# Normalising the last 17 layer norms on GpSimd in a four-layer gated kernel

## The reference, cut to what matters

```python
def _layernorm(x, axis=-1, eps=1e-05):
    m = jnp.mean(x, axis=axis, keepdims=True)
    v = jnp.var(x, axis=axis, keepdims=True)
    return (x - m) / jnp.sqrt(v + eps)

x = x + jnp.tanh(g_xattn[0]) * _L0_xattn_ref(_layernorm(x, axis=-1), ...)   # gated by token range
x = x + jnp.tanh(g_ffn[0]) * _L0_ffn_ref(_layernorm(x, axis=-1), ...)       # 64 experts, top 4, and shared
x = x + jnp.tanh(g_xattn[1]) * _L1_xattn_ref(_layernorm(x, axis=-1), ...)   # mLSTM heads
x = x + jnp.tanh(g_ffn[1]) * _L1_ffn_ref(_layernorm(x, axis=-1), ...)       # low rank, 8 experts
x = x + jnp.tanh(g_xattn[2]) * _L2_xattn_ref(_layernorm(x, axis=-1), ...)   # attention with a cache
x = x + jnp.tanh(g_ffn[2]) * _L2_ffn_ref(_layernorm(x, axis=-1), ...)       # ternary weights, 8-bit tokens
x = x + jnp.tanh(g_xattn[3]) * _L3_xattn_ref(_layernorm(x, axis=-1), ...)   # attention kept to the 54 best
x = x + jnp.tanh(g_ffn[3]) * _L3_ffn_ref(_layernorm(x, axis=-1), ...)       # ternary weights, relu squared
```

## Time and profile before

| what | value |
|---|---|
| median of 3 runs | 614.92 us (612.87 to 615.05) |
| profiled execution, its own time | 614.48 us |
| its span, first to last instruction | 612.7 us |
| TensorE (PE) busy | 459.0 us, 75% |
| VectorE (DVE) busy | 361.6 us, 59% |
| ScalarE (ACT) busy | 231.9 us, 38% |
| GpSimd (POOL) busy | 170.6 us, 28% |
| mean granted TensorE clock | 0.852 |

### The profile page before, as it was taken

The page is one execution under the profiler, slowest core; times in us unless marked ns, Lnnn a source line. Parts: engine busy times, 40 slices in busy tenths (PEclk is TensorE's granted clock), DMA queues, the critical chain, the costliest instruction groups (busy, mean ns, idle before and its releaser), DMA issues.

```text
span 612.7 us, 7209 instructions
## 1 busy us (share of the span) xinstructions
PE 459.0 (75%) x2538; PEld 332.1 (54%) x2546; DVE 361.6 (59%) x1021; ACT 231.9 (38%) x405; POOL 170.6 (28%) x165
## 2 busy tenths in 40 slices
PE   1999986949999026768987099999997676754664
PEld 0788862318887013435654067788873364633442
DVE  6463367961113363976555354422479999999844
ACT  1200036242243313345432032223467662334775
POOL 4000017783803675340425650000011010000200
PEclk9999969888999665769878569999999987966877
DMA  8860502113991510010001000000000000000001
GB/s 279 264 267 2 205 0 82 32 39 113 350 311 58 173 37 12 7 40 29 2 1 50 20 2 0 1 0 1 1 1 1 0 2 0 2 0 1 18 18 34
DMA packets 25124, 37.59 MB, mean 61 GB/s; under 512 B 5678, under 2 KB 20148, under 8 KB 25088
## 3 DMA queue, kind: packets, MB, share of 16 engines
q1 hardware_dynamic: 22016, 33.38, 16.0%
q0 software_dynamic: 3072, 3.75, 2.1%
HBM read 32.32 MB, written 9.44 MB: 68 GB/s over the span
## 4 chain that ended last, share of the span: by engine, by line
PE 45%; DVE 30%; POOL 10%; issue 7%; ACT 5%; DMA 2%; POOLq 0%; DVEq 0%; ACTq 0%
PE bank L1427 5%; PE bank L1514 5%; PE bank L1437 5%; PE bank L1747 3%; POOL ar L557 3%; POOL xg_rows L515 3%; PE bank L1536 3%; DVE top L1103 2%; DVE big L1100 2%; DVE HN L606 2%; PE bank L1761 2%; PE bank L1785 2%; PE bank L1769 2%; DVE bnst L596 2%; PE bank L1801 2%
## 5 line engine op out<-in xcount | busy, mean ns | idle before, releaser
L470 POOL TENSOR_TENSOR rstd<-ve,neghalf 128x2 f32<-128x2 f32 x32 | 24.9, 779 | 265.1 <-DVE ve L601 265.0
L515 POOL DMA_INDIRECT xg_rows<-HN,slot x32 | 33.1, 1033 | 21.8 <-DVE slot L727 12.6
L774 DVE TENSOR_TENSOR he<-sil,bank 64x64 f32<-64x64 f32 x32 | 7.0, 218 | 52.9 <-ACT sil L1192 52.7
L916 DVE TENSOR_TENSOR SH<-bank,HM 128x512 f32<-128x512 f32 x32 | 22.0, 689 | 24.4 <-ACT HM L1268 10.0
L557 POOL TENSOR_TENSOR ar<-ar,neghalf 128x32 f32<-128x32 f32 x4 | 21.7, 5431 | 41.1 <-DVE ar L880 41.1
L1468 PE MATMUL bank<-HT,SH 128*128 128x512 f32 x64 | 33.0, 674 | 0.0
L606 DVE TENSOR_SCALAR HN<-X,mv,rstd 128x256 f32<-128x256 f32 x64 | 26.9, 462 | 9.8 <-POOL rstd L470 9.6
L1514 PEld LDWEIGHTS bank<-ph,big 128*128 128x128 f32 x256 | 31.3, 193 | 1.3 <-issue 0.4
L1268 ACT ACTIVATE HM<-bank 128x512 f32<-128x512 f32 x32 | 19.1, 598 | 32.5 <-PE bank L1623 27.9
L1427 PE MATMUL bank<-HM,CT 128*128 128x256 f32 x128 | 30.2, 398 | 1.2 <-DVE HM L630 1.2
L1514 PE MATMUL bank<-ph,big 128*128 128x64 f32 x256 | 30.6, 273 | 0.0
(11 more groups left out here) (356 smaller groups left out, 1173.1 us busy)
## 6 DMA issues: line engine op xcount, KB each, us to landing
big<-in_ew SPq DMA_DIRECT2D x16, 768.0 KB, 6.4
xg_rows<-zer SPq DMA_DIRECT2D x1, 2048.0 KB, 8.4
ph<-xg_rows SPq DMA_DIRECT2D x16, 128.0 KB, 4.2
y_rows<-ph SPq DMA_DIRECT2D x16, 128.0 KB, 2.7
X<-in_x SPq DMA_DIRECT2D x4, 256.0 KB, 6.6
CT<-in_ctxT SPq DMA_DIRECT2D x1, 1024.0 KB, 7.6
CN<-in_ctx SPq DMA_DIRECT2D x1, 1024.0 KB, 11.6
ar<-in_q2g SPq DMA_DIRECT2D x1, 1024.0 KB, 4.8
```

The costliest lines, as they stand in the source:

```text
L470: pool.tensor_tensor(rstd[:, b, :], ve[:, b, :], neghalf[:, 0:TB], ALU.pow)\
L515: pool.indirect_dma_start(out=xg_dram, out_offset=bass.IndirectOffsetOnAxis(slot[:, t, k:k + 1], 0), in_=HN[:, t, :], in_offset=None, boun ...
L916: dve.tensor_tensor(cs[:, g, :], bank[i % 3][:], dcs[:, i % 2, :], ALU.mult).then_inc(s["s_cs"], 1)
```

## The change

The two tensor_scalar instructions of each of the 17 planned norms leave VectorE's program and stand in GpSimd's, directly behind the power whose result they use. GpSimd waits for its own power (`s_lnrstd`) before them and counts a new semaphore `s_gnorm`. TensorE's `turn` and VectorE's `quantise_tokens` wait for `s_gnorm` in place of `s_norm`. The steps `turn1`, `norm4` and `norm6` have no part of VectorE any more, so their nine turns leave VectorE's string in `TURNS_OF`; the order of all the other steps, on every engine, stays the same (the strings are only broken at other places). The load of `ctx` gives up its semaphore and counts as the fourth of the group `shared`, at its old place in the queue. The 15 norms ahead of the plan stay on VectorE.

```diff
--- before.py
+++ after.py
@@ -45,20 +45,20 @@
         (("in2a", "TVS"), ("in2b", "TVS"), ("round2", "VS"), ("turn2", "TS"), ("out2", "TV" if j < TB - 1 else "TVG"))]
 FFN3 = [((name, j), engines) for j in range(TB) for name, engines in
         (("in3", "TVS"), ("round3", "VS"), ("turn3", "TS"), ("out3", "TV"))]
-STEPS = ([("heads", "VG"), ("turn1", "TVS"), ("route1", "TVS"), ("low1", "TV"), ("lowturn1", "TS"), ("lowout1", "TVG"),
-          ("norm4", "TVS"), ("keys2", "TS"), ("values2", "TS"), ("scores2", "TVS"), ("probs2", "TS"), ("mix2", "TS"),
+STEPS = ([("heads", "VG"), ("turn1", "TS"), ("route1", "TVS"), ("low1", "TV"), ("lowturn1", "TS"), ("lowout1", "TVG"),
+          ("norm4", "TS"), ("keys2", "TS"), ("values2", "TS"), ("scores2", "TVS"), ("probs2", "TS"), ("mix2", "TS"),
           ("project2", "TVG"), ("norm5", "VSG"), ("turn5", "TS")] + FFN2 +
-         [("norm6", "TVS"), ("queries3", "TS"), ("scores3", "TVS"), ("clip3", "VS"), ("probs3", "TS"), ("mix3", "TS"),
+         [("norm6", "TS"), ("queries3", "TS"), ("scores3", "TVS"), ("clip3", "VS"), ("probs3", "TS"), ("mix3", "TS"),
           ("project3", "TVG"), ("norm7", "VSG"), ("turn7", "TS")] + FFN3)
 
 TURNS_OF = {
-    "T": ("021012130230130201230201320103123012313010232303112201023031031212013203231010302121313002"
-             "3023231110033311202012103130210213232323232"),
-    "V": ("012303123001132203312003101220301321021032013012312031023121302303213103032101201313021201"
-             "0130123232323232"),
-    "S": ("012130230012302012010312312301030231302101220132130321032013013212310203023101310102323231"
-             "310003230111201213013021032123232323232"),
-    "G": "3012300112233012300113322",
+    "T": ("02101213023013020123020132010312301231301023230311220102303103121201320323101030212131300230"
+          "23231110033311202012103130210213232323232"),
+    "V": ("01230123013203120031012203013210210320130123120312312302303110303210120131302120101301232323"
+          "23232"),
+    "S": ("01213023001230201201031231230103023130210122013213032103201301321231020302310131010232323131"
+          "0003230111201213013021032123232323232"),
+    "G": ("3012300112233012300113322"),
 }
 
 
@@ -336,7 +336,7 @@
                  "s_hcp s_hr16 s_v16 s_r16 s_hh s_wif0 "
                  "s_l1 s_nm1 s_ex1 s_ha s_hm1 s_hmt s_hmc s_y1 "
                  "s_qk s_qk2 s_v s_v2 s_sc2 s_nm2 s_ex2 s_pt2 s_ptc2 s_qs s_xf s_sq s_o2 s_oc2 s_y2 "
-                 "s_asum s_wsc s_wr s_qw s_mixe "
+                 "s_gnorm s_asum s_wsc s_wr s_qw s_mixe "
                  "s_qn s_qt s_qc s_gu s_gs s_hr s_rh s_hm s_hq s_hqt s_hqc s_yq s_xq "
                  "s_q3 s_qc3 s_sc3 s_sl3 s_coef s_m3 s_ex3 s_p3 s_pt3 s_ptc3 s_o3 s_oc3 s_y3").split()
         s = {n: sem(n) for n in dict.fromkeys(names)}
@@ -349,8 +349,8 @@
 
 
         GROUPS = {"x0": ["x0"], "x1": ["x1"], "x2": ["x2"], "x3": ["x3"], "g": ["g"], "tokb": ["tokb"],
-                  "ctxT": ["ctxT"], "ctx": ["ctx"],
-                  "router": ["router", "rbias"], "shared": ["sg", "su", "sd"],
+                  "ctxT": ["ctxT"],
+                  "router": ["router", "rbias"], "shared": ["sg", "su", "sd", "ctx"],
                   "small": ["wi", "wf", "lnsc", "mix", "lg"] + [f"{g}{b}" for g in ("bi", "bf") for b in range(B)],
                   "late": ["la", "lb", "wq", "wk", "wv", "wo", "w3q", "w3o"],
                   "q2g": ["q2g"], "q2u": ["q2u"], "q2d": ["q2d"], "q3a": ["q3a"], "q3b": ["q3b"]}
@@ -568,7 +568,13 @@
                     ln_rstd(b, 3 * B + b + 1)
             for step, b in PLAN["G"]:
                 if step in STATS:
+                    n = nth("G", STATS, step, b)
                     ln_rstd(b, BEFORE + nth("V", STATS, step, b))
+                    pool.wait_ge(s["s_lnrstd"], BEFORE + n)
+                    for j in range(TB):
+                        last = pool.tensor_scalar(HN[:, TB * b + j, :], X[:, TB * b + j, :], mv[:, b, j, 0:1],
+                                                  rstd[:, b, j:j + 1], ALU.subtract, ALU.mult)
+                    last.then_inc(s["s_gnorm"], 1)
                 if step in QUANTS:
                     pool.wait_ge(s["s_xf"], nth("S", QUANTS, step, b))
                     pool.tensor_scalar(XQ[:, b], HN[:, TB * b:TB * (b + 1), :], -MAGIC, 1.0, ALU.add, ALU.mult)\
@@ -829,7 +835,7 @@
 
             def centred_values():
 
-                landed(dve, "ctx")
+                landed(dve, "shared")
                 dve.wait_ge(s["s_ey"], ST)
                 values = CN[:].rearrange("p t (h c) -> p (t h) c", c=DH)
                 link(dve.tensor_reduce(vmean, values, AX.X, ALU.add))
@@ -1002,8 +1008,6 @@
             for step, b in PLAN["V"]:
                 if step == "heads":
                     heads_add(b)
-                if step in NORMS:
-                    ln_norm(b, BEFORE + nth("G", STATS, STATS[NORMS.index(step)], b))
                 if step == "route1":
 
                     dve.wait_ge(s["s_l1"], nth("T", ["route1"], step, b))
@@ -1047,7 +1051,7 @@
                     add_scaled(b, bank_b(b))
                     ln_stats(b)
                 if step in ("norm5", "norm7"):
-                    dve.wait_ge(s["s_norm"], BEFORE + nth("V", NORMS, step, b))
+                    dve.wait_ge(s["s_gnorm"], nth("G", STATS, STATS[NORMS.index(step)], b))
                     quantise_tokens(b, ("norm5", "norm7").index(step))
                 if step[0] in ("in2a", "in2b"):
                     n = ("in2a", "in2b").index(step[0])
@@ -1401,9 +1405,8 @@
         def _(pe):
             def turn(u, dst, b=None, ln=None):
 
-                if b is None:
-                    b, ln = u % B, u + 1
-                pe.wait_ge(s["s_norm"], ln)
+                pe.wait_ge(s["s_norm" if b is None else "s_gnorm"], u + 1 if b is None else ln)
+                b = u % B if b is None else b
                 for k in range(KD):
                     for j in range(TB):
                         last = pe.transpose(dst[:, S * k + P * j:S * k + P * (j + 1)],
@@ -1731,7 +1734,8 @@
             pe.wait_ge(s["s_freea"], read_before(len(ORDER) - 1)[1])
             for step, b in PLAN["T"]:
                 if step in TURNS:
-                    turn(None, bank_b(b) if step == "turn1" else bank_a(b), b, BEFORE + nth("V", NORMS, step, b))
+                    turn(None, bank_b(b) if step == "turn1" else bank_a(b), b,
+                         nth("G", STATS, STATS[NORMS.index(step)], b))
                 if step == "route1":
                     if b == B - 1:
                         pe.wait_ge(s["s_ht"], 2 * B + nth("S", TURNS, "turn1", b))
```

## The result

| | before | after |
|---|---|---|
| median | 614.92 us (612.87 to 615.05, 4 runs) | 625.12 us (624.47 to 625.81, 4 runs) |
| ratio | 1 | 1.0179, 95% interval 1.0155 to 1.0202 |
| profiled execution | 614.48 us, span 612.7 | 625.81 us, span 624.1 |
| VectorE busy | 361.6 us | 350.4 us |
| GpSimd busy | 170.6 us | 212.3 us |

The change makes the kernel 1.8% slower by the ratio, 10 us by the medians. Of the runs that follow, one of the kernel before (640.72 us) and one of the last experiment (905.64 us) were slow ones and count in no median or ratio. The forecast was 614.2 us with 76% for no difference. The rival that it held at 7%, GpSimd's pair as the wait, is what happened.

The account below looks back on a forecast made before the run. TensorE was taken to bound 350 to 445 us, VectorE 445 to 583, nobody the last 30. Terms 1.5 - 1.1 - 1.3 + 0.4 - 0.1 - 0.4 + 0.3 = -0.7 gave 614.2 us, range 611.0 to 617.7.

Parts of the forecast that it names:

- GpSimd's pair as the wait: Seven norms have their result waited for: 7 us per us of pair, zero at 1.15, +3.1 at 1.6; chance 7%.
- Part 1: norm5 of b=2 and 3, norm7 of b=3 and 2: VectorE waits for the result, 4 x 0.38 = +1.5 us.
- Part 2: norm6 of b=0 and 1: VectorE's L1055 can start earlier without the pair ahead of it, -1.1 us together.
- Part 3: norm6 of b=2 and 3: both pairs leave full VectorE work, 0.64 us each, -1.3 us.
- Part 4: GpSimd's pairs meet VectorE's tensor_scalars: norm6 of b=3 +0.4 us, norm7 of b=0 -0.1, norm7 of b=1 -0.4.
- the rival of the locks: Exclusion between GpSimd and VectorE always costs: Part 4 at its dear ends, sum +0.8, 615.7 us; chance 22%.
- Part 5: TensorE's stretch up to 445 us: only norm4 of b=2 is close, TensorE stands idle +0.3 us (0 to 0.7).
- the clock rival: Shifted idle gaps could move an edge of TensorE's granted clock, 3 us either way; chance 4% up, 4% down.
- VectorE's time is what counts: VectorE's full stretch loses 8.1 + 2.5 us; with two thirds kept, 7.0, the kernel takes 607.9 us; chance 8%.

Follow-up runs that it names:

- the last experiment: Against the kernel before: norm6 of b=2 and 3 and norm7 of b=1 alone moved to GpSimd, with negated mean and addition; 613.39 us, ratio 0.9995.

## Why the prediction was wrong, step by step

**The step that failed is a term that was mis-sized: "That is 0.55 each, 1.1 a pair; consecutive instructions will overlap a little, so I take 1.05."** It measured 1.226 each and 2.43 to 2.44 a pair, outside the range of 0.82 to 1.4. The 0.83 ns an element came from GpSimd instructions of the right kind and type, but with other arithmetic: L574 of the earlier trace rows adds and multiplies, L528 of the earlier trace rows takes a minimum and a maximum, and no row of before subtracts on GpSimd. The fixed time (0.20 + 0.14 us forecast, 0.37 measured) and the charge for operands in it (140 ns forecast, 151 measured) were right. The text said that it would be wrong "if GpSimd's instruction is over 0.8 us", and that was the case.

**Part 1** had the mechanism right: four waits, each paid whole, 0.08 + pair - 0.75. With 2.43 it gives 1.76 each; measured 1.78, and 0.42 for a forecast of 0.38 where the pair is 1.09.

**Part 2** was right with a pair of 1.09 (-1.1 as forecast) and came to 0.0 with 2.43. Its sentence on TensorE's turn of b=0, "some 0.4 later; the step behind it [...] hides it", holds for 0.4 only: the turn came 1.8 us late and the step behind paid.

**Part 3** was right in both: -0.64 and -0.53 for 0.64 each.

**Part 4** took half a blocked pair, +0.4, for norm6 of b=3. It measured +0.15, with GpSimd's pair even 2.48 us long (last section). Norm7 of b=0 and b=1 came out at -0.2 and -0.6 with the short pair (forecast -0.1 and -0.4), and +1.0 and +0.8 with the long one. So the rival of the locks, with +1.05 for norm6 of b=3, falls.

**Part 5** was right in place: +0.4 with the short pair, +1.7 with the long.

**The rival** said 7 us for each us of a pair, zero at 1.15. At 2.43 that is 7 x 1.28 = +9.0. Between the kernels with addition and subtraction, whose pairs differ by 1.35 us, the seven places of the table differ by 5.4 + 1.3 + 1.2 + 1.4 = 9.3, or 6.9 for each us: this slope is shown. Its chance of 7% rested on one row, "a 128x512 on GpSimd takes 0.66 us", which was true and did not bear on it. What the rival did not have is norm6 of b=0 (+1.0) and the clock at 469 to 477 us. The latter is the clock rival in small: +1.1 in the profiled execution of after, +1.0 in that of all seventeen with the negated mean, nothing in the other two with the slow subtraction at all seventeen places (constants, and one instruction of 512), and its cause was not tested. The 0.9 us before 390 us belong to no part of the change that was tested; in the profiled executions of the other kernels the same point stands 0.3 to 5.0 us early, over code that is the same as in after.

The rival "VectorE's time is what counts" falls: VectorE lost 11.2 us of busy time, and even with the short pair the kernel is no faster.

That the kernel with the addition comes out at -0.6 where -0.7 was forecast is in part luck: its terms sum to -0.8, and the -0.5 ahead of them and the +0.7 behind them, for which the forecast had nothing, nearly cancel.

## What to carry to other kernels

Before an instruction is moved to another engine, look for a row of that engine with the same arithmetic, and not only with the same type and shape; if there is none, bounds taken from other arithmetic are not bounds, and where several places wait for the result the price counts once for each. Move what the giving engine has other work behind: norm6 of b=2 and 3 brought 0.6 and 0.5 us even at 2.4 us a pair, while a norm whose result is the next thing in the queue paid the whole difference. A gain of 2 us ahead of stages that the clock governs should not be booked before those stages are seen to run at the same clock.

## What the runs showed of the hardware that was not expected

**GpSimd subtracts at a quarter of the rate at which it adds.** tensor_scalar in float32, per-partition operands, 128x256: (x - a) * b 1226 ns, (x + a) * b 566 ns; 3.35 against 0.83 ns an element. With constants the subtraction is 1075 ns. Only the form with the subtraction first, in float32, was tried. VectorE shows no such thing in before: its pairs with the subtraction take 0.73 to 0.75 us. The cause inside GpSimd was not looked for. The Trainium skill (GPSIMD Engine Reference, section Elementwise — side-by-side cycle accounting) has 1.03 cycles an element for loop bodies with k ≤ 2, read here as at most two operations, and about 2.6 with two inputs; at its 1.2 GHz the first is 0.86 ns, an estimate from the page's figures. The addition, at 0.83 ns, agrees with it; 3.35 ns would be 4.0 such cycles, above both, and the measurement decides.

**The exclusion of the two engines was weaker than at 266 us.** The timelines of after, GpSimd and then VectorE, where norm6 of b=3 meets `scores3`:

```profile
523.83 2.48 POOL L575 TENSOR_SCALAR HN<-X,mv,rstd 128x256 f32<-128x256 f32 x2
```

```profile
523.82 0.36 DVE L1092 TENSOR_SCALAR top<-top,nmax 128x8 f32<-128x8 f32 x2
524.09 0.76 DVE L1094 TENSOR_SCALAR big<-big,nmax 128x256 f32<-128x256 f32 x2
524.88 0.09 DVE L1104 MATCH_VALUE_LOAD big<-top,big 128x8 f32 x1
```

The same VectorE pair in before, with GpSimd idle:

```profile
517.25 0.61 DVE L1090 TENSOR_SCALAR big<-big,nmax 128x256 f32<-128x256 f32 x2
```

VectorE's two 128x256 started 0.26 us into GpSimd's pair and were through by 524.85, inside its first instruction, for 0.15 us more than the 0.61 that they take alone; GpSimd paid 0.05. With the addition the same meeting cost 0.15 and 0.22. With one GpSimd subtraction of 128x512 VectorE's pair took 0.97 us, 0.36 more than alone, so the delay grew with the size of GpSimd's instruction. Yet at 266 us a VectorE pair of the same size waited for both of GpSimd's 128x2048. The Trainium skill (SBUF — State Buffer, section Who interferes with whom) has the later one of such instructions blocked for the whole of the earlier; the rows at 266 us agree; those at 524 us don't, if the two tensor_scalars there are of that kind, which no row says. What tells the two apart was not tried and stays open.
